# Pairwise field products of a recommendation tower: eight fields of the first chunk taken from whole tables by one-hot products, and the weights' transfers issued without waits

## The reference, cut to what matters

```python
# 32 tables of 1000 to 125000 rows, 64 wide; ids (512, 32); all float32
e = stack([tbl_f[ids[:, f]] for f in range(32)], axis=1)     # (512, 32, 64)
p, q = e[:, ids_x], e[:, ids_y]                              # the 496 pairs x < y
z = einsum('bpj,bpj->bp', einsum('bpi,pij->bpj', p, w), q)   # w (496, 64, 64)
h = concatenate([z, dense_ctx], axis=1)                      # (512, 512)
h = maximum(h @ W_top1 + b_top1, 0)
h = maximum(h @ W_top2 + b_top2, 0)
y = h @ W_top3                                               # (512, 1)
```

## Time and profile before

| | |
|---|---|
| median of 3 runs | 218.34 us |
| the profiled execution's own time | 218.69 us |
| its span, first to last instruction | 216.9 us |
| busy PE, DVE, ACT, POOL | 191.2, 172.7, 153.7, 153.7 us |
| mean granted TensorE clock | 0.992 |

### The profile page before, as it was taken

How to read it: one execution, slowest core, us unless ns; L and a number is a source line. 1 busy time by engine, 2 the same in 40 slices (tenths; PEclk the granted TensorE clock), 3 DMA queues, 4 the chain that set the end, 5 groups by cost and what they waited for, 6 DMA issues and landing times.

```text
span 216.9 us, 6361 instructions
## 1 busy us (share of the span) xinstructions
PE 191.2 (88%) x2142; PEld 130.4 (60%) x2142; DVE 172.7 (80%) x157; ACT 153.7 (71%) x1178; POOL 153.7 (71%) x192
## 2 busy tenths in 40 slices
PE   0119869989998989999999999999999999999985
PEld 0017446534765654875876756675587745687874
DVE  0004686898999979999997999899999966999811
ACT  2000267599999989999989679997798883619401
POOL 4777777777777777777777777777788878885200
PEclk9999997999999999999999999999999999999999
DMA  5676657557111111111111111111100000000000
GB/s 186 255 228 232 233 193 237 201 168 282 27 30 29 27 30 26 27 33 26 24 34 29 24 30 28 29 30 27 26 21 14 9 2 0 3 2 3 5 0 0
DMA packets 6434, 15.23 MB, mean 70 GB/s; under 512 B 2689, under 2 KB 2945, under 8 KB 5250
## 3 DMA queue, kind: packets, MB, share of 16 engines
q1 hardware_dynamic: 2306, 10.62, 13.6%
q0 software_dynamic: 4096, 4.20, 9.3%
HBM read 14.82 MB, written 0.00 MB: 68 GB/s over the span
## 4 chain that ended last, share of the span: by engine, by line
PE 68%; POOL 8%; DVE 8%; issue 6%; ACT 4%; DMA 3%; DVEq 0%
PE pu L531 23%; PE pu L523 22%; PE pz L544 11%; POOL emb L313 8%; PE pt L551 5%; ACT turned L342 4%; DVE turned L425 3%; DVE prod L443 3%; PE pt L563 2%; DMA emb<-in_tbl,idx 2%; PE pu L551 1%; DVE prod L439 1%; DVE zB L451 1%; PE pu L491 1%; PE pt L573 1%
## 5 line engine op out<-in xcount | busy, mean ns | idle before, releaser
L313 POOL DMA_INDIRECT emb<-in_tbl,idx x128 | 121.2, 947 | 41.2 <-issue 29.8
L342 ACT ACTIVATE turned<-turned 128x64 f32<-128x64 f32 x560 | 134.0, 245 | 1.8 <-DVE turned L425 1.8
L342 ACT ACTIVATION_READ_ACCUMULATOR turned<-turned 128x1 f32 x560 | 107.3, 192 | 0.0
L425 DVE TENSOR_TENSOR turned<-pu,emb 128x1024 f32<-128x1024 f32 x64 | 76.0, 1217 | 9.8 <-PE pu L523 9.8
L443 DVE TENSOR_TENSOR prod<-pu,eT 128x1024 f32<-128x1024 f32 x48 | 57.1, 1217 | 22.7 <-PE pu L531 22.5
L531 PEld LDWEIGHTS pu<-eT,ws 64*128 64x128 f32 x1024 | 64.3, 193 | 16.6 <-issue 11.6
L531 PE MATMUL pu<-eT,ws 64*128 64x128 f32 x1024 | 68.7, 283 | 4.0 <-ACT eT L332 1.7
L523 PE MATMUL pu<-ws,eT 64*128 64x512 f32 x256 | 67.7, 630 | 2.4 <-DVE prod L443 0.8
L523 PEld LDWEIGHTS pu<-ws,eT 64*128 64x128 f32 x256 | 22.5, 192 | 21.5 <-issue 20.1
L332 ACT COPY eT<-pu 128x128 f32<-128x128 f32 (+1 forms) x28 | 11.1, 398 | 34.1 <-PE pu L491 34.0
L299 POOL TENSOR_TENSOR turned<-turned 128x512 f32<-128x512 f32 (+4 forms) x50 | 30.3, 607 | 6.6 <-DVE turned L425 3.3
(11 more groups left out here) (27 smaller groups left out, 29.7 us busy)
## 6 DMA issues: line engine op xcount, KB each, us to landing
ws<-in_w SPq DMA_DIRECT2D x8, 1024.0 KB, 4.8
emb<-in_tbl,idx POOLq DMA_INDIRECT x128, 2.4
w1s<-in_w SPq DMA_DIRECT2D x1, 1024.0 KB
zT<-in_dense SPq DMA_DIRECT2D x1, 512.0 KB, 3.3
w2s<-in_w SPq DMA_DIRECT2D x1, 512.0 KB
idx<-in_ids SPq DMA_DIRECT2D x1, 64.0 KB, 2.0
identity<-in_ident SPq DMA_DIRECT2D x1, 64.0 KB, 1.9
w3s<-in_w SPq DMA_DIRECT2D x1, 1.0 KB
```

Of the source, the lines that this page charges most:

```text
L313: nc.gpsimd.indirect_dma_start(out=emb[:, c % EC, x, :], out_offset=None, in_=tables[x], in_offset=bass.IndirectOffsetOnAxis(ap=idx[:, c, ...
L342: i = nc.scalar.activation(t, t, ACT.Copy, accum_out=zB[:, b // NT % 2, b % NT * 16 + v:b % NT * 16 + v + 1])
L425: nc.vector.tensor_tensor(turned[:, b % RB, :, :].rearrange("p (x f) i -> p x (f i)", x=2), u.rearrange("p x s i -> p x (s i)"), e, ALU.mu ...
```

## The change

Eight fields with tables of 1000 rows are moved to the places 8 to 15 of the field order, which are pairs 4 to 7 (`FIELD_AT`; the host permutes tables, ids and weight blocks to fit). In the first chunk these eight are not gathered. SP loads the eight tables whole, each as 125 partitions of 8 rows (250 KB), and a list of their ids, repeated on 125 partitions. DVE compares the list with the row numbers (L510, eight instructions on 125 x 1024) and so gets columns with a single one in each. TensorE multiplies table by columns (L548, 64 products, 16 for a pair), which gives the pair already turned over, and ACT copies it. POOL has 24 gathers in the first chunk in place of 32. The tables and columns lie in parts of `turned` and `prod` that are not used yet.

All groups of pairs 0 to 7 now stand ahead of step 0, in the order 4, 5, 0, 1, 6, 7, 2, 3. SP issues the list, the tables and then the eight weight transfers, and waits for nothing between them. The tables that set the order are all new, and so is the share of the row sums: ACT has 38 turned units in place of 35, DVE 17 in place of 19, POOL 9 in place of 10.

```diff
+HOT_FIELDS = (1, 3, 7, 14, 15, 19, 20, 26)
+HP, HJ = 125, 8
+HOT = range(8, 16)
+FIELD_AT = _REST[:8] + list(HOT_FIELDS) + _REST[8:]
+def is_hot(c, k):
+    return c == 0 and 2 * k in HOT
-TURNED = [2, 3, 5, 9, 10, 11, 12, 13, 18, 19, 20, 21, 22, 26, 28, 29]
+TURNED = [2, 3, 4, 5, 8, 10, 12, 14, 18, 20, 21, 23, 24, 26, 27, 29]
-W_AT_ONCE = 2
+FIRST = (4, 5, 0, 1, 6, 7, 2, 3)
+GROUPS = [(0, k, 1) for k in FIRST + tuple(range(8, KP))]
-X_AT = [[-1, -1, -1, -1, 1, 2, 3, 4, 6, 7, 10, 12, 15, 16, 19, 24], [28, 33, 39, 48], [60, 61, 71, 74], [91, 92, 98, 109]]
+X_AT = [[-1, -1, -1, -1, -1, -1, -1, -1, 0, 5, 7, 9, 11, 13, 17, 20], [27, 31, 38, 45], [54, 63, 67, 80], [83, 93, 103, 109]]
-SUMS_AT = ((3, 10, 11, 18, 20, 22, 28), (1, 6, 7, 11, 21, 22, 24, 25), (1, 7, 15, 19, 26), (0, 1, 10, 27, 31))
+SUMS_AT = ((5, 7, 9, 10, 17, 20, 23, 27, 31), (0, 5, 6, 12, 22, 30), (3, 10, 13, 26), (1, 7, 10, 13, 27, 31))
...
             sp.dma_start(idx[:], ids).then_inc(s_idx, 16)
-            sp.dma_start(identity[:], ident).then_inc(s_ident, 16)
+            sp.dma_start(hot_list(), hot_ids.broadcast_to([HP, len(HOT) * P])).then_inc(s_hot_ids, 16)
+            sp.dma_start(rows_at[0:HP, :], hot_rows).then_inc(s_hot_rows, 16)
+            for i, x in enumerate(HOT):
+                sp.dma_start(hot_table(i), tables[x].rearrange("(p j) e -> p j e", j=HJ)).then_inc(s_hot[i // 2], 16)
+                if i == 3:
+                    sp.dma_start(identity[:], ident).then_inc(s_ident, 16)
             for g in range(NU // WU):
-                if g >= W_AT_ONCE:
-
-                    sp.wait_ge(s_emb[2 * (g - W_AT_ONCE) + 1], 16 * 2)
                 sp.dma_start(ws[:, g * WU:(g + 1) * WU, :, :].rearrange("p u s i -> p (u s i)"),
...
             for c in range(BCH):
                 for x in range(FIELDS):
+                    if is_hot(c, x // 2):
+                        continue
...
+            for i in range(len(HOT)):
+                if i >= 4:
+
+                    dve.wait_ge(xt_ready, hot_group(i - 4) + 1)
+                at = rows_at[0:HP, :]
+                nc.vector.tensor_tensor(hot_columns(i).rearrange("p (j b) -> p j b", j=HJ),
...
+                                        ALU.is_equal).then_inc(ones_ready, 1)
...
+                if is_hot(c, k):
+                    i = 2 * k - HOT[0]
+                    pe.wait_ge(ones_ready, i + 2)
+                    pe.wait_ge(s_hot[i // 2], 16 * 2)
+                    for j in range(HJ):
+                        for h in range(2):
+                            mm = nc.tensor.matmul(pu[EMB * h:EMB * (h + 1), FILL["x", g] % UR, 0, 0, :], hot_table(i + h)[:, j, :],
+                                                  hot_columns(i + h)[:, j * P:(j + 1) * P], start=(j == 0), stop=(j == HJ - 1))
+                    mm.then_inc(xt_ready, 1)
+                    return
```

More of the change, by code:

```diff
@@ L32 @@
 KP = FIELDS // 2
+HOT_FIELDS = (1, 3, 7, 14, 15, 19, 20, 26)
+HOT_ROWS = 1000
+HP, HJ = 125, 8
+assert HP * HJ == HOT_ROWS
+HOT = range(8, 16)
+_REST = [f for f in range(FIELDS) if f not in HOT_FIELDS]
+FIELD_AT = _REST[:8] + list(HOT_FIELDS) + _REST[8:]
+def is_hot(c, k):
+    return c == 0 and 2 * k in HOT
 UNITS = []
@@ L50 @@
 assert NU == 32 and NT == 16 and all(UNITS[u][0] == "four" for u in TURNED)
+assert all(2 * (UNITS[u][2] + i) not in HOT for u in TURNED for i in range(4))
 assert ZCH * P == FIELDS * (FIELDS - 1) // 2 + DENSE
-TURN_AT = [[2, 3, 7, 9, 10, 11, 12, 16, 17, 18, 20, 21, 22, 29, 30, 31], [5, 6, 7, 10, 11, 12, 13, 15, 18, 20, 22, 23, 25, 26, 29, 31], [2, 3, 7, 8, 9, 10, 11, 14, 17, 18, 23, 26, 27, 29, 30, 31], [0, 5, 6, 10, 11, 12, 13, 14, 15, 16, 17, 18, 19, 20, 24, 26]]
+TURN_AT = [[0, 2, 4, 6, 8, 9, 10, 13, 14, 17, 19, 21, 24, 27, 30, 31], [4, 5, 6, 7, 11, 14, 16, 17, 18, 20, 21, 22, 25, 29, 30, 31], [2, 6, 7, 9, 12, 13, 15, 17, 18, 19, 21, 22, 23, 25, 26, 30], [1, 4, 5, 6, 9, 10, 11, 14, 18, 19, 20, 22, 23, 25, 26, 27]]
 ORDER = []
@@ L113 @@
 WU = 4
-W_AT_ONCE = 2
 XN = [1, 4, 4, 4]
-GROUPS = [(c, k, XN[c]) for c in range(BCH) for k in range(0, KP, XN[c])]
+FIRST = (4, 5, 0, 1, 6, 7, 2, 3)
+assert XN[0] == 1
+GROUPS = [(0, k, 1) for k in FIRST + tuple(range(8, KP))]
+GROUPS += [(c, k, XN[c]) for c in range(1, BCH) for k in range(0, KP, XN[c])]
 NG = len(GROUPS)
-X_AT = [[-1, -1, -1, -1, 1, 2, 3, 4, 6, 7, 10, 12, 15, 16, 19, 24], [28, 33, 39, 48], [60, 61, 71, 74], [91, 92, 98, 109]]
-MLP_AT = [(7, 15, 27, 37, 54), (8, 9, 34, 38, 45), (14, 15, 19, 23, 27)]
+X_AT = [[-1, -1, -1, -1, -1, -1, -1, -1, 0, 5, 7, 9, 11, 13, 17, 20], [27, 31, 38, 45], [54, 63, 67, 80], [83, 93, 103, 109]]
+MLP_AT = [(14, 19, 26, 39, 51), (13, 16, 22, 29, 36), (10, 13, 17, 21, 25)]
 X_STEPS = [at for of_chunk in X_AT for at in of_chunk]
@@ L160, with dlrm_tower @@
 SUMS[NS] = list(range(_a, BCH * NA))
-Z_LATE = [2, 1, 1, 116]
+Z_LATE = [3, 1, 4, 291]
 Z_OUT = [Z_LATE[c] + min(t for t in SUMS if (c + 1) * NA - 1 in SUMS[t]) for c in range(BCH - 1)]
-def dlrm_tower(nc, tables, ids, w, dense, w1, b1, w2, b2, w3, ident, out):
+def dlrm_tower(nc, tables, ids, hot_ids, hot_rows, w, dense, w1, b1, w2, b2, w3, ident, out):
     with ExitStack() as ctx:
@@ L175, in sem @@
             return ctx.enter_context(nc.semaphore(name))
+        rows_at = sb("rows_at", [P, HJ], I32)
         idx = sb("idx", [P, BCH, FIELDS], I32)
@@ L202, in dlrm_tower @@
         s_emb = [sem(f"emb_in{i}") for i in range(BCH * KP)]
+        s_hot_ids = sem("hot_ids_in")
+        s_hot_rows = sem("hot_rows_in")
+        s_hot = [sem(f"hot_tables_in{i}") for i in range(len(HOT) // 2)]
+        ones_ready = sem("ones_ready")
         s_w = [sem(f"w_in{i}") for i in range(NU // WU)]
@@ L250, in turned_over, with hot_table, hot_columns, hot_list @@
                 .rearrange("p h (i b) -> p i h b", b=BH)
+        def hot_table(i):
+            return turned[0:HP, 6 + i // 2, 8 * (i % 2):8 * (i % 2) + HJ, :]
+        def hot_columns(i):
+            return prod[0:HP, 5 + i % 4, :, :, :].rearrange("p x s b -> p (x s b)")
+        def hot_list():
+            return prod[0:HP, 4, :, :, :].rearrange("p x s b -> p (x s b)").bitcast(I32)
+        def hot_group(i):
+            return GROUP_OF[0, HOT[i] // 2]
         def slot_free(engine, fill):
@@ L331, in copy_x @@
                     act.wait_ge(mult_done, (c - EC + 1) * NU)
+                if is_hot(c, k):
+                    nc.scalar.copy(eT[:, c % EC, k, :], pu[:, FILL["x", g] % UR, 0, 0, :]).then_inc(xt_read, 1)
+                    return
                 nc.scalar.copy(eT[:, c % EC, k:k + n, :].rearrange("p i (h b) -> p i h b", h=2),
@@ L457, in z_rows @@
                 nc.vector.tensor_tensor(zT[:, 0:ZA, cols(c)], pz[:], zT[:, 0:ZA, cols(c)], ALU.add).then_inc(z_out, 1)
+            dve.wait_ge(s_hot_ids, 16)
+            dve.wait_ge(s_hot_rows, 16)
+            for i in range(len(HOT)):
[3 more added lines that the diff above has]
+                nc.vector.tensor_tensor(hot_columns(i).rearrange("p (j b) -> p j b", j=HJ),
+                                        bass.AP(hot_list().tensor, hot_list()[:, i * P:(i + 1) * P].offset,
+                                                [hot_list().ap[0], [0, HJ], [1, P]]),
+                                        bass.AP(at.tensor, at.offset, [at.ap[0], [1, HJ], [0, P]]),
+                                        ALU.is_equal).then_inc(ones_ready, 1)
             for t in range(NS):
@@ L650 @@
     arrays = {
-        "ids": np.asarray(inputs["ids"]).reshape(BCH, P, FIELDS).transpose(1, 0, 2),
+        "hot_ids": np.asarray(inputs["ids"])[:P, list(HOT_FIELDS)].T.reshape(1, len(HOT) * P),
+        "hot_rows": np.arange(HOT_ROWS, dtype=np.int32).reshape(HP, HJ),
+        "ids": np.asarray(inputs["ids"])[:, FIELD_AT].reshape(BCH, P, FIELDS).transpose(1, 0, 2),
         "w": w_blocks.reshape(P, NU, 4, P),
@@ L668 @@
     out = nc.dram_tensor("out_y", (BATCH, 1), F32, kind="ExternalOutput").ap()
-    dlrm_tower(nc, [aps[f"tbl_{f}"] for f in range(FIELDS)], aps["ids"], aps["w"], aps["dense"],
+    dlrm_tower(nc, [aps[f"tbl_{f}"] for f in FIELD_AT], aps["ids"], aps["hot_ids"], aps["hot_rows"], aps["w"], aps["dense"],
                aps["w1"], aps["b1"], aps["w2"], aps["b2"], aps["w3"], aps["ident"],
```

4 lines of the change are left out of this document (2 added, 2 removed).

## The result

The changed kernel takes **225.98 us** (median of 4 runs, 225.47 to 226.58), the kernel before on the same chip 218.38 (4 runs): ratio 1.035, interval 1.0319 to 1.0383. It is slower by 7.6 us. The forecast was 222.0, with a range up to 225.5: the sign was right, the size (3.7 us) half of what came. The profiled execution took 225.61 us, its span is 223.8.

What follows compares the result with a forecast made beforehand. Gathers and a landing were taken to bound the kernel to 31.7 us, then mostly TensorE. First chunk's end +4.9, later part -1.2, sum +3.7 on the 218.34 median gave 222.0 us, range 208.5 to 225.5.

Steps and rivals of the forecast that it cites:

- The five engines: Transfers of 125 rows are dealt to five DMA engines, 25 rows each; chance 0.70.
- Rival 1: Tables go over all 16 engines: step 0 at 18.5 us, time 210.4 us; chance 0.27 together with Rival 2.
- When tables and first weights land: With 0.62 MB on each of five engines, last tables land at 26.4 us, first weights at 28.9.
- Step 0: First unit on TensorE starts at about 29.3 us in place of 16.06, behind last tables, products and weights.
- First multiply: DVE's first multiply comes 2.1 us after step 0, at 31.4 us, since TensorE runs cold at first.
- Chunk 0: First chunk on DVE takes 41.5 us from the first multiply, ending at 72.9 where it was 68.01.
- The rest: Later, TensorE-bound part gets 1.2 us shorter, as sums and a group of four pairs move ahead.
- the sign of being right: A DMA share of 0.3 to 0.4 once other engines are through, between 15 and 27 us or later.
- ACT's eleven more us: Three more turned units on ACT, 11.5 us of work, cost 0, up to 2 us if a buffer frees late.
- The waits: SP's weight waits for gathers (32.5 us in its queue) delay no unit; dropping them gives nothing by itself.
- Rival 2: DVE comparisons on two SBUF operands block POOL's gathers: 0 on five engines, 213 to 215 us on 16; with Rival 1 0.27.
- Rival 4: Five engines, but first chunk at the 36 to 68 us pace and chilled TensorE: 224 to 226 us; no separate chance.

Runs made afterwards that it cites:

- e1_even: Changed kernel with each table in two transfers, of 112 and 13 rows, and the id list on 128 partitions: 213.24 us, ratio 0.974.
- e2_tables_first: Changed kernel, but SP waits for all eight tables before it issues the first weights: 223.06 us, ratio 1.0188.
- s5: Kernel before with only SP's waits for gathers between weight transfers taken out, third run of it: 218.81 us, ratio 1.0055.
- s1_aligned: s8 with each table as 7 rows on each of 128 partitions and the last 104 rows one each: 211.52 us, ratio 0.9712.
- e4: Changed kernel with the eight comparisons replaced by memsets to zero: 226.75 us (one run).
- s7: e1_even with identity issued ahead of the id list and a column buffer of its own for every comparison: 215.17 us, ratio 0.9874.
- s8: s7 with the row numbers copied to PSUM and read from there by the comparisons: 211.46 us, ratio 0.97.

## Why the prediction was right, and where it failed

- **The five engines**: right. 3606 packets, as forecast. Rival 1, the tables over all engines, didn't happen; e1_even shows what it would have given.
- **When tables and first weights land**: the step that failed. It priced 0.62 MB on each of five engines at 22.5 to 25.9 KB/us, from stretches in which all transfers were dealt in 128 rows, and took the weights on the other eleven engines for harmless to the tables. Measured: 84 ns for 2048 bytes (24.4 KB/us, as assumed) only until the weights flow, then about 140 ns (14.6 KB/us). The last table row is down at 29.7 us where 26.4 was forecast, the first weights at 33.4 (14.32 and 19.1 to landing) for 28.9. e2_tables_first shows the step to be the cause: without the overlap the pace holds, and step 0 is 4.1 us sooner.
- **Step 0**: 34.29 for 29.3, +5.0. Of these 3.3 are the landing; 1.0 lies between the last row and TensorE's start; the last 32 products took 3.18 us, 99 ns each, where those at 23.89 took 62, since the granted clock had fallen to 0.50, and with what follows them that is 0.7 more than forecast. The forecast's own terms (26.4 + 2.8 + 0.26) already make 29.5, and pairs 2 and 3 come on top; it took 29.3.
- **First multiply** 1.3 us behind it (2.1 forecast; the granted clock was back at 1.00 from 34.65 us on), -0.8. **Chunk 0**: 42.2 for 41.5, +0.7, inside the 41 to 43 asked for. **The rest**: 146.0 for 148.9 before, -2.9 where -1.2 was forecast; no run separates where the other 1.7 comes from. Sum 3.7 + 5.0 - 0.8 + 0.7 - 1.7 = 6.9, which is 225.61 - 218.69.
- **SP's queue**: the forecast let the issues pass in no time. They were held up (6.66 us for four tables), so identity, issued at 5.14, let the first product start at 16.81. It cost nothing here, since the last pair of tables is later still; in e1_even it was the reason for 10.88. It also softened the step that failed, by luck: the weights, which the forecast had on the other engines from the start, flow only from 16.9 us, when some 108 of each engine's 200 table rows were down. At 140 ns those rows would have taken 6 us more (an estimate from the packets). So the sign of being right, a share of 0.3 to 0.4 after 15 us, didn't come: the share is 0.41 ahead of 16 us and 1.03 to 1.05 from 20 to 28.
- **ACT's eleven more us**: 0, as forecast; ACT ended no long wait, and the rest got shorter.
- **The waits**: forecast at nothing by themselves. s5 has +1.1 us (+1.7 at the same clock), through late gathers; how much of it is in the changed kernel, whose gathers have slack, no run tells.
- **Rival 1** gave 210.4 from step 0 at 18.5; e1_even had 21.78 and 213.24, s1_aligned 19.43 and 211.52. **Rival 2** gave 0 with five engines (e4: right) and 213 to 215 with sixteen (s7: 215.17; e1_even, with three slow gathers: 213.24). **Rival 4**'s time, 224 to 226, held the result, but in the main by a cause that isn't its own: the chunk's pace lost 0.7 us, and the clock 1.2 us ahead of step 0, which the forecast's 2.8 us for those products had mostly in it.
- **The range** ended at 225.5, 0.5 us below the result. The forecast's likeliest case went up to 226, which would have held it; why the range stopped short of that, it doesn't say. Its slow end took 22.5 KB/us, which isn't the lowest rate in the earlier trace rows of a stretch with weights: 16 to 22 us have 223/16/0.72 = 19.4, and by that (an estimate) the first weights land at 35. No row of before had two kinds of deals at once, and the 14.6 KB/us measured then are below these too.

Still open: where rows of different deals get in each other's way. The runs show that the rate falls with transfers of 125 and 112 rows and less with 128. The Trainium skill (page "DMA: Bandwidth & Descriptors", section "The descriptor swizzle") gives each engine of a 128-partition transfer partitions that lie on one write port of SBUF, its own; shares of 25 or 7 partitions next to each other would then meet other engines' ports. e1_even, e2 and s1 don't contradict it, and no run measures a port by itself, or which partitions a share of 25 or 7 rows has.

## What to carry to other kernels

Choose the outer count of a transfer so that all sixteen engines share it; here 125 rows cost 13 us against 112 + 13 (with the id list on 128). Where you can, lay it on all 128 partitions: that gave a higher rate here, though no time. Price a transfer that runs on few engines with the others both idle and full: the price of a row differed by 5/3. And before you fill a waiting DVE with instructions on two SBUF operands, look at what POOL has to issue meanwhile; one operand from PSUM kept every gather at 0.95 us, though the whole kernel gained by it on one chip of three. And compare runs of the same granted clock: one stretch of 3.4 us at half clock was worth about 2 us in the kernel before.

## What the runs showed of the hardware

- 125 rows run on 5 engines, 112 on 16, 13 on 13 and 104 on 13 (packet counts 3606, 3812 and 4682).
- With all engines busy, 252 to 278 GB/s in nearly every stretch in which table rows of 125 or 112 partitions flow (320 once, s8 from 6 to 8 us), 332 to 368 with 128, 391 to 422 for weights alone.
- A 2048-byte row on five engines takes 84 ns while the others are nearly idle and about 140 beside weights; the weights' 8192-byte packets take 452 to 501 ns then, and alone 309 (before) to 326 (after the change).
- An issue on SP waits once its engines are behind: 6.66 us for four tables on five engines, 0.32 to 0.43 for each table transfer of e1_even, s7 and s8, dealt over sixteen and thirteen.
- A gather's issue on POOL grows from 0.95 to 1.97 us beside a DVE comparison with both operands in SBUF (most of them, not each: 0.95 at 7.91 us after the change, 0.99 at 8.17 in s7), and stays at 0.95 with one in PSUM.
- A gather landed after 6.3 to 7.2 us beside a flood of weights, where the earlier trace rows have 4.85 before.
- TensorE's granted clock fell to 0.50 for 3.4 us after it had waited 4.80 us for a table (after the change) and 2.42 and 0.46 us for gathers (s7), and stayed at 1.00 from the first product to the last unit in e1_even and s8.
